# Heads of six stages, and the order of the head sums in attention, in a one-core vision block

## The reference

```python
x = x + conv(_gn(x), ...)          # u = silu(xn @ W_u.T), v = silu(xn @ W_v.T), y = tno2d(v, rpe_coeffs(...)), (u*y) @ W_o.T + b_o + shortcut
t = _to_tokens(x)                  # 8 x 3136 tokens x 256
t = t + attention(_ln_t(t), W_qkv, W_proj, b_proj)
t = t + ffn(_ln_t(t), fc1, fc2)    # Haar split, interpolation, fc1, gelu, fc2, inverse split
# attention, per image and head of 32 channels
q, k = sigmoid(q), sigmoid(k); v = v / (scale * c // H)
k_sum, q_sum = k.sum(tokens), q.sum(tokens)
sink_incoming   = 1 / (((q + EPS) * (k_sum + EPS)).sum(-1) + EPS)
source_outgoing = 1 / (((k + EPS) * (q_sum + EPS)).sum(-1) + EPS)
conserved_sink   = ((q + EPS) * ((k * source_outgoing).sum(tokens) + EPS)).sum(-1) + EPS
conserved_source = clip(((k + EPS) * ((q * sink_incoming).sum(tokens) + EPS)).sum(-1) + EPS, -1, 1)
kv  = einsum(k, v * softmax(conserved_source) * tokens)
out = einsum(q, kv) * sink_incoming * sigmoid(conserved_sink)
```

## Time and profile before

| | us |
|---|---|
| three runs | 5514.95, 5515.36, 5510.22; median 5514.95 |
| the profiled execution | 5516.2, span 5514.4 |
| PE busy | 5263.6, 95% of the span |
| DVE busy | 3927.7, 71% |
| ACT busy | 2458.8, 45% |
| POOL busy | 2490.1, 45% |
| DMA | 782.55 MB, mean 142 GB/s |
| mean granted clock of PE | 0.975 of full |

### The profile page before, as it was taken

The page is one execution under the profiler, slowest core; times in us unless marked ns, Lnnn a source line. Parts: engine busy times, 40 slices in busy tenths (PEclk is TensorE's granted clock), DMA queues, the critical chain, the costliest instruction groups (busy, mean ns, idle before and its releaser), DMA issues. The chain is left out here.

```text
span 5514.4 us, 88804 instructions
## 1 busy us (share of the span) xinstructions
PE 5263.6 (95%) x26936; PEld 3667.2 (67%) x26936; DVE 3927.7 (71%) x6061; ACT 2458.8 (45%) x4678; POOL 2490.1 (45%) x1383
## 2 busy tenths in 40 slices
PE   8999899997999999999989999999799999987999
PEld 6777655554555555555547777777666666665999
DVE  5666566666999999999976666666455555554887
ACT  4444477874333333333335555555522222211555
POOL 0000044444999999999975555555111111111332
PEclk9999999998999999999999999999899999998999
DMA  3222167775444444444446666666433333322443
GB/s 107 87 87 70 50 198 217 217 219 163 150 150 150 150 150 150 150 150 150 150 142 177 202 197 195 204 192 204 135 100 100 97 102 95 95 81 85 124 122 113
DMA packets 349116, 782.55 MB, mean 142 GB/s; under 512 B 43433, under 2 KB 147845, under 8 KB 339460
## 3 DMA queue, kind: packets, MB, share of 16 engines
q1 hardware_dynamic: 326596, 703.91, 43.1%
q10 hardware_dynamic: 22400, 77.08, 4.0%
HBM read 420.49 MB, written 360.38 MB: 142 GB/s over the span
## 5 line engine op out<-in xcount | busy, mean ns | idle before, releaser
L889 POOL TENSOR_TENSOR co_prod<-co_cross 111x512 f32<-111x512 f32 x448 | 849.8, 1897 | 0.0
L823 ACT ACTIVATE co_y_out<-co_y_ps 112x512 f32<-112x512 f32 x448 | 267.9, 598 | 927.5 <-PE co_y_ps L769 922.7
L886 POOL TENSOR_TENSOR co_prod<-co_direct 111x512 f32<-111x512 f32 x448 | 577.1, 1288 | 204.2 <-PE co_y_ps L769 115.5
L863 DVE TENSOR_TENSOR co_direct<-co_v_ps,co_spec 111x1024 f32<-111x1024 f32 x448 | 543.3, 1213 | 92.0 <-PE co_v_ps L135 87.8
L1953 POOL TENSOR_TENSOR at_t<-at_t,at_p_bias 112x1024 f32<-112x1024 f32 x56 | 134.3, 2408 | 973.6 <-DMA at_t<-t_tiles 973.6
L865 DVE TENSOR_TENSOR co_cross<-co_v_ps,co_spec 111x1024 f32<-111x1024 f32 x448 | 541.3, 1208 | 0.0
L135 PE MATMUL co_v_ps<-co_v_high,co_col_fwd_high 112*111 112x512 f32 x896 | 506.1, 565 | 1.5 <-DVE co_cross L865 1.4
L767 PE MATMUL co_y_ps<-co_prod,co_col_inv 111*112 111x512 f32 x896 | 458.2, 592 | 0.0
L769 PE MATMUL co_y_ps<-co_prod,co_col_inv 111*112 111x512 f32 x896 | 457.5, 592 | 0.1
L2117 ACT ACTIVATE at_qk_t<-at_bank_ps 128x448 f32<-128x448 f32 x224 | 121.8, 544 | 564.8 <-PE at_bank_ps L135 564.8
L843 DVE TENSOR_TENSOR co_v_low<-co_v_in,co_v_high 112x1024 fp32r<-112x1024 f32 x224 | 372.4, 1663 | 0.2
(11 more groups left out here) (267 smaller groups left out, 14173.8 us busy)
## 6 DMA issues: line engine op xcount, KB each, us to landing
v_rows<-pr_rows_out SPq DMA_DIRECT2D x56, 1792.0 KB, 8.2
co_v_in<-v_rows SPq DMA_DIRECT2D x448, 224.0 KB
y_rows<-co_y_out SPq DMA_DIRECT2D x448, 224.0 KB
mx_y_in<-y_rows SPq DMA_DIRECT2D x224, 448.0 KB, 5.5
kr_x_in<-x SPq DMA_DIRECT2D x56, 448.0 KB, 3.7
kern_rows<-kr_rows_out SPq DMA_DIRECT2D x28, 896.0 KB, 4.7
pr_x_in<-x SPq DMA_DIRECT2D x112, 224.0 KB
mx_x_in<-x SPq DMA_DIRECT2D x56, 448.0 KB, 5.2
```

What stands on the lines that cost most here:

```text
L823: nc.scalar.activation(y_out[:, b, :], y_ps[b % 2][:2 * SIDE, :], ACT.Copy).then_inc(y_ready, 1)
L863: nc.vector.tensor_tensor(direct[b % 2][:], v_ps[b % 2][:POINTS, :], spec[i][:, :2 * WIDE], ALU.mult).then_inc(real_terms, 1)
L886: nc.gpsimd.tensor_tensor(prod[b % 2][:, :WIDE], direct[b % 2][:, :WIDE], direct[b % 2][:, WIDE:], ALU.subtract).then_inc(real_ready, 1)
L889: nc.gpsimd.tensor_tensor(prod[b % 2][:, WIDE:], cross[b % 2][:, :WIDE], cross[b % 2][:, WIDE:], ALU.add).then_inc(combined, 1)
```

## The change

The lines of attention stand some 20 further down in the file after. In each head the loads are put in another order and count on semaphores of their own, and the engines wait for them one by one where they use them:

- Kernel rows: the split of w_out (ACT, DVE) comes behind the first mean, square and roots; PE waits for the low part of w_out first where it is used.
- Project: `ident` and `w_v` are issued ahead of the first image; ACT splits w_v before the squares.
- Columns: the two loads of taps are issued ahead of the three constants.
- Mix: `ident`, then `w_u`, the second image, the biases, `w_o` last. The first image is normalised on DVE instead of POOL. PE turns the first image after `ident`, and w_o is split after the first x.
- Attention: PE, DVE and ACT wait for the raw q/k weights only; the other constants are waited for later.
- ff: the stats are issued first, then fc1 and interp, the first tile, the rest. ACT takes the root ahead of the two copies of fc1.

In attention's images three things move. The token sums and `at_sel` become a function `sum_tokens`, which runs for the next image in the output part, behind the last residual but one and ahead of its statistics. The first head sums write another bank of PSUM (`flow_ps = bank[6]`), wait neither for `t2_ready` nor behind unit 0, and five units instead of three follow them; the pieces have nine units instead of ten. Unit 18 goes behind the second gram step, unit 19 one step later.

```diff
@@ -448,8 +449,6 @@
-                act.wait_ge(tail_in, 16 * len(tail_loads))
-                nc.scalar.activation(w_out[0][:], raw_out[:], ACT.Copy).then_inc(high_consts, 1)
@@ -490,6 +489,8 @@
+                act.wait_ge(tail_in, 16 * len(tail_loads))
+                nc.scalar.activation(w_out[0][:], raw_out[:], ACT.Copy).then_inc(high_consts, 1)
@@ -706,9 +707,9 @@
+                load_taps(sp, 0, 0)
...
-                load_taps(sp, 0, 0)
@@ -967,6 +969,8 @@
+                sp.dma_start(ident[:], d["ident"]).then_inc(ident_in, 16)
+                sp.dma_start(raw_v[:], d["w_v"]).then_inc(weights_in, 16)
@@ -1126,6 +1131,10 @@
+                act.wait_ge(weights_in, 16)
+                nc.scalar.activation(w_v[0][:], raw_v[:], ACT.Copy).then_inc(high_consts, 1)
+                act.wait_ge(xt_mm, 1)
+                high_half(0, 0)
@@ -1207,9 +1211,11 @@
+                dve.wait_ge(weights_in, 16)
...
+                dve.wait_ge(consts_in, 16 * len(loads))
@@ -1330,13 +1337,13 @@
-                sp.dma_start(raw_u[:], d["w_u"]).then_inc(consts_in, 16)
-                sp.dma_start(raw_o[:], d["w_o"]).then_inc(consts_in, 16)
+                sp.dma_start(ident[:], d["ident"]).then_inc(ident_in, 16)
+                sp.dma_start(raw_u[:], d["w_u"]).then_inc(u_in, 16)
+                load_x(0, 1, first=True)
...
+                sp.dma_start(raw_o[:], d["w_o"]).then_inc(o_in, 16)
                 for u in range(2):
-                    if u:
-                        load_x(0, u, first=True)
@@ -1382,14 +1389,16 @@
-                    pool.wait_ge(scaled_x, g + 1)
+                    pool.wait_ge(scaled_x, g)
+                    if g == 1:
+                        pool.wait_ge(gx_ready, 1)
...
-                        pool.wait_ge(consts_in, 16 * (len(loads) + 2))
+                        pool.wait_ge(consts_in, 16 * len(loads))
@@ -1513,15 +1521,17 @@
-                pe.wait_ge(consts_in, 16 * (len(loads) + 2))
-                pe.wait_ge(low_consts, len(splits))
-                pe.wait_ge(gaps_clear, 4)
-                pe.wait_ge(y_clear, 2)
+                pe.wait_ge(ident_in, 16)
...
+                pe.wait_ge(low_consts, 1)
+                pe.wait_ge(gaps_clear, 4)
...
+                pe.wait_ge(consts_in, 16 * len(loads))
+                pe.wait_ge(y_clear, 2)
+                pe.wait_ge(low_consts, len(splits))
@@ -1622,12 +1632,13 @@
-                act.wait_ge(consts_in, 16 * (len(loads) + 2))
                 act.wait_ge(eps_set, 1)
-                for raw, split in splits:
-                    nc.scalar.activation(split[0][:], raw[:], ACT.Copy).then_inc(high_consts, 1)
+                act.wait_ge(u_in, 16)
+                nc.scalar.activation(w_u[0][:], raw_u[:], ACT.Copy).then_inc(high_consts, 1)
...
+                act.wait_ge(o_in, 16)
+                nc.scalar.activation(w_o[0][:], raw_o[:], ACT.Copy).then_inc(high_consts, 1)
@@ -1749,15 +1760,24 @@
+                each = [TILE, TILES, CH]
+                scale0, shift0 = (gn_rows[:TILE, 0, r * CH:(r + 1) * CH].unsqueeze(1).to_broadcast(each) for r in range(2))
+                dve.wait_ge(x_loaded[0], 16)
+                nc.vector.tensor_tensor(gx[0][:], x_in[0][:], scale0, ALU.mult).then_inc(scaled0, 1)
+                dve.wait_ge(scaled0, 1)
+                nc.vector.tensor_tensor(gx[0][:], gx[0][:], shift0, ALU.add).then_inc(gx_ready, 1)
...
-                dve.wait_ge(consts_in, 16 * (len(loads) + 2))
-                for i, (raw, split) in enumerate(splits):
-                    dve.wait_ge(high_consts, i + 1)
-                    nc.vector.tensor_tensor(split[1][:], raw[:], split[0][:].bitcast(F32), ALU.subtract).then_inc(low_consts, 1)
+                dve.wait_ge(u_in, 16)
+                dve.wait_ge(high_consts, 1)
+                nc.vector.tensor_tensor(w_u[1][:], raw_u[:], w_u[0][:].bitcast(F32), ALU.subtract).then_inc(low_consts, 1)
...
+                dve.wait_ge(o_in, 16)
+                dve.wait_ge(high_consts, 2)
+                nc.vector.tensor_tensor(w_o[1][:], raw_o[:], w_o[0][:].bitcast(F32), ALU.subtract).then_inc(low_consts, 1)
+                dve.wait_ge(consts_in, 16 * len(loads))
@@ -1809,7 +1829,8 @@
-        flow_ps = kept_ps = z_ps = kv_out_ps = bank[2]
+        flow_ps = bank[6]
+        kept_ps = z_ps = kv_out_ps = bank[2]
@@ -2037,18 +2057,17 @@
-                    units(0)
-                    pe.wait_ge(t2_ready, b * SUMS)
...
-                    units(1, 2, 3)
+                    units(0, 1, 2, 3, 4)
...
-                        units(*range(4 + piece * 10 // PIECES, 4 + (piece + 1) * 10 // PIECES))
+                        units(*range(5 + piece * 9 // PIECES, 5 + (piece + 1) * 9 // PIECES))
+                    pe.wait_ge(t2_ready, b * SUMS)
@@ -2058,18 +2077,17 @@
+                    turn_keys(0)
+                    turn_keys(1)
...
-                    turn_keys(0)
-                    turn_keys(1)
-                    units(18)
...
-                        if n == TILES:
-                            units(19)
+                        if n in (1, TILES + 1):
+                            units(18 + n // TILES)
@@ -2165,6 +2183,7 @@
+                act.wait_ge(split_consts, 3)
@@ -2177,8 +2196,6 @@
-                dve.wait_ge(consts_in, 16 * (len(loads) + 1))
-                dve.wait_ge(cleared, 1)
@@ -2188,38 +2205,40 @@
-                def back(im, front, beyond):
...
-                    dve.wait_ge(qt_ready, (b + 1) * UNITS)
...
+                def sum_tokens(im):
+                    dve.wait_ge(qt_ready, (im.b + 1) * UNITS)
+                def back(im, front, beyond):
...
@@ -2327,6 +2346,8 @@
+                            if front and j == CHUNKS - 1:
+                                sum_tokens(ahead)
@@ -2380,9 +2404,9 @@
-        loads = [(fc1_raw, "fc1"), (interp, "interp"), (fc1_bias, "fc1_bias"), (fc2, "fc2"), (fc2_bias, "fc2_bias"),
-                 (pair_tok, "pair_tok"), (ident, "ident")]
-        ALL_LOADS = len(loads) + BATCH
+        first_loads = [(fc1_raw, "fc1"), (interp, "interp")]
+        loads = [(pair_tok, "pair_tok"), (fc1_bias, "fc1_bias"), (fc2, "fc2"), (fc2_bias, "fc2_bias"), (ident, "ident")]
+        stats_in, weights_in = T.sem("stats_in"), T.sem("weights_in")
@@ -2402,12 +2426,14 @@
+                for b in range(BATCH):
+                    sp.dma_start(stats[:, b], d["t2_stats"][b]).then_inc(stats_in, 16)
+                for tile, name in first_loads:
+                    sp.dma_start(tile[:], d[name]).then_inc(weights_in, 16)
+                sp.dma_start(t2[0][:], d["t2_tiles"][0]).then_inc(loaded[0], 16)
...
-                for b in range(BATCH):
-                    sp.dma_start(stats[:, b], d["t2_stats"][b]).then_inc(consts_in, 16)
-                for u in range(2):
-                    sp.dma_start(t2[u][:], d["t2_tiles"][u]).then_inc(loaded[u], 16)
+                sp.dma_start(t2[1][:], d["t2_tiles"][1]).then_inc(loaded[1], 16)
@@ -2505,18 +2531,18 @@
+                pe.wait_ge(consts_in, 16 * len(loads))
...
-                act.wait_ge(consts_in, 16 * ALL_LOADS)
+                act.wait_ge(var_ready, 1)
+                nc.scalar.activation(root[:], var[:], ACT.Sqrt).then_inc(rooted, 1)
...
-                act.wait_ge(var_ready, 1)
-                nc.scalar.activation(root[:], var[:], ACT.Sqrt).then_inc(rooted, 1)
+                act.wait_ge(consts_in, 16 * len(loads))
```

65 lines of the change are left out of this document (33 added, 32 removed).

## The result

The changed kernel took 5418.6 us (median of 4 runs, 5414.53 to 5428.35) against 5513.57 before (4 runs); the ratio is 0.9834, 95% interval 0.9821 to 0.9847. Five more runs in a later session gave 5413.49 (5406.24 to 5420.72), ratio 0.9823 (0.9811 to 0.9836); all nine have the median 5418.1. The forecast was 5415, with 5396 to 5444 around it.

The account below looks back on a forecast made before the run. PE, busy 95% of the span, was taken as the bound, with gains only from 251 us idle and slow clock. Attention -74 and heads -25.9 sum to -99.9; 5516.2 less that, less 1.25, gives 5415 us, range 5396 to 5444.

Parts of the forecast that it names:

- Head sums at E, sums behind another cover: Attention: head sums start at E (end of an image's last output matmul); earlier token sums cost nothing, 0.9 us being hidden.
- E to the second head sums: Attention images: 36.2 to 36.9 us instead of 44.9; 8.0 taken for each of six images, -48 in all.
- from there on DVE bounds: Attention pieces from the spread's start: VectorE's 28 steps, low parts, lag and token sums take 25 to 25.7 us.
- Rival 2: Attention: cast and low part of the flows still collide with GpSimd, 2.5 in six images: +15, 5430 us; chance 0.06.
- Unit 18: Attention: placed after two gram steps, it waits 0 to 0.4 instead of 1.90, -10.5 us, plus -11 of clock.
- The clock: Attention, behind unit 18's wait: about half of 24 us at half speed comes back, -11 us, bounds 0 and 12.
- Heads: The six stage heads, with loads and splits reordered: -25.9 us in sum.
- Mix: Mix head: VectorE normalises the first image, PE turns it without waiting for w_o: -6.5 us, bounds -8 and -4.
- Columns: Columns head: reordering five loads gains 0 us, as the same bytes precede the last landing; bounds -4 and +1.
- 1 (no clock back): Attention: clock falls anyway, pieces keep pace; the 11 us stay lost, each image gains 6, not 8; chance 0.20.
- 3 (heads give nothing): All heads: the loads' bandwidth, not their order, bounds them, so nothing is gained: +26, 5441 us; chance 0.05.
- 4: Attention: PE stays at half clock for the whole piece stage, +7.3 per image, 5540 us; chance 0.03.

Follow-up runs that it names:

- the heads run: Two runs: kernel before with only the changed kernel's six heads, 5486.73 us; changed kernel with columns, ff and mix heads done otherwise, 5412.0 us.
- the last run: Changed kernel with columns loads of 111 rows in two, third chunk's low part ahead of the scratch steps, and three extra matmuls: 5413.31 us, ratio 0.9812.

## Why the prediction was right

The forecast of 5415 was 3.6 us under the median of its runs, 1.5 above that of the second session. That the median came so near is in part luck, since single runs of the program lie 22 us apart; that the parts came out is not. Point by point:

- *Head sums at E, sums behind another cover.* Right: they start at E + 0.3 to 0.5 in images 1 to 7. One statement in it was wrong: the three operations were to cost 0.9. Of them the second took 2.09 for 0.17, beside the bias addition that began at 4108.55:

```profile
4108.83 2.09 DVE L2226 TENSOR_SCALAR at_total_eps<-at_total 128x4 f32<-128x4 f32 x1
```

  It was covered, as PE had until E. The 0.3 us are no cost of it: without the additions, where the operation takes 0.17, the head sums start at E + 0.31 too.
- *E to the second head sums.* -8.0 forecast; image by image -7.5 in the first profile (37.8 for 45.3, counted from the start of the last output matmul) and -8.8 in the second (36.5). The working behind it had two errors that went against each other. The spread starts at E + 12.1, for 11.6 counted so, 0.5 late. And "from there on DVE bounds" holds with 24.0 to 24.9 in the second profile, not 25 to 25.7. The forecast had named a mean clock under 0.9 as a sign of being wrong; of images 1 to 6 it was met in image 2 of the first profile (0.88), in none of the second.
- *Rival 2* was priced at 15 us for six images and given 0.06. Its place was wrong (cast and low part of the flows: quiet), its mechanism is at work one step on. Its size, 10 to 16 us on the median run, is what removing the additions shows; that takes in everything that the additions touch, and against the second session it is not clear of the interval. I costed the piece stage's own low parts at 2.2 with "may collide" left out of the range's reasons; the row with its 7.5 us of additions over E + 12 to 20 said that the low part behind the sixth scratch step, at E + 17, falls under them.
- *Unit 18.* Forecast -21.5, measured -21.3 and -21.8 in the traces, 18 to 23 by undoing it. The forecast counted the stretches as 6.8, 6.8 and five of 3.4 or less; the trace has five in all, the two and three of 3.4, which make its 24 us.
- *The clock.* The -11 behind unit 18 came: the stretches there are gone in both profiles. What the forecast did not have is that stretches come and go in the pieces and in the first and last image, 15 us between the two profiles. That is 15 of the 22 by which they differ (-88 and -110).
- *Heads.* -25.9 forecast, -27 to -28 measured alone. *Mix* came out smaller: -3.6, below its own bounds of -4 to -8, and -5.8, for -6.5. In the first profile the first turn came 5.6 earlier in the stage, for 6.0, and the gate's product 4.6, for 6.0. Ahead of it ScalarE and DVE had split w_u (DVE's low part of x waited for w_u's); in the second profile, with the same order, both came 6.2 to 6.5 earlier:

```profile
2871.74 1.23 DVE L1774 TENSOR_TENSOR mx_w_u_low<-mx_raw_u,mx_w_u_high 128x1024 fp32r<-128x1024 f32 x1 [1.42 <-ACT mx_w_u_high L1637]
2873.55 1.01 PE L1428 MATMUL mx_turn_ps<-mx_ident,mx_gx 112*128 112x112 f32 x4 [2.10 <-DVE mx_x_t_low L1655]
2877.96 3.07 DVE L1779 TENSOR_TENSOR mx_w_o_low<-mx_raw_o,mx_w_o_high 128x1024 fp32r<-128x1024 f32 x1 [2.16 <-ACT mx_w_o_high L1641]
```

  The lines are of the first profile. The low part of w_o, 3.07 beside GpSimd, stood ahead of the gates; moving it behind them gained nothing in the heads run. Why the two profiles differ here is open.
- *Columns.* 0 forecast, -0.1 and -1.4 measured, and for the reason given: the order of the loads does not matter where the same slow transfers must all land. What the forecast did not draw from it is that splitting them was the edit to make.
- *Rivals 1, 3 and 4.* 1 (no clock back) is refuted by the traces behind unit 18 and by the time; that the clock can fall in the pieces, as it said, is so in some images of some executions. 3 (heads give nothing) is refuted by the heads run. 4 was seen in one image of the last run.

## What to carry to other kernels

A wait of PE can cost its length and as much again, in clock and in collisions of what it moves to a later place: putting a wait of 2.3 us back into seven images cost 27 to 32 us and not 16. Look for what makes a wait long only sometimes, such as two engines' operations that meet when a load lands late: part of the run-to-run spread comes from there. When an edit takes one operation out of such a meeting, look which one it moves in. The head that waited for loads of 111 rows was helped by splitting them into 96 and 15 (first product 9.8 earlier, 4.2 kept by the stage), not by reordering them.

## What was not expected of the hardware

- A DVE operation of 128 x 4 elements took 2.09 us beside a GpSimd addition, against 0.17 alone; the reciprocal of 128 x 448, 2.95 us, was never lengthened.
- PE kept the half clock for 30.7 us while it was busy for all of them, after one wait of 2.35 (best version, image 5); in image 2 of the changed kernel it was back after 10.2.
- Two matmul waits of 0.73 and 0.80 in a row were followed by the half clock in three images of one profile and not in three others, and a single one of 1.9 was not in four of seven (unit 18 put back). The waits alone are not enough to tell whether the clock will fall.
